# First attention stage: row-softmax results summed into the column-softmax bank by identity products, one copy and one output projection instead of two

## What is computed

```
w = (x @ W.T) split into heads; q, k, v = rms_norm(w) * g1, g2, g3
att   = q k^T / sqrt(d)
score = softmax(att, axis=-1) + softmax(att, axis=-2)
y     = score @ v, heads joined
x     = x + y @ W
```

## Time and profile before

| what | value |
|---|---|
| median of 3 runs | 331.37 us (329.57 to 331.48) |
| the profiled execution, its own time | 331.63 us |
| its span, first to last instruction | 329.6 us |
| around the span | 2.0 us |
| mean granted TensorE clock | 0.891 |
| block 1's loop in the span | about 46 to 145.4 us |

### The profile page before, as it was taken

How to read it: one execution, slowest core, us unless ns; L and a number is a source line. 1 busy time by engine, 2 the same in 40 slices (tenths; PEclk the granted TensorE clock), 3 DMA queues, 4 the chain that set the end, 5 groups by cost and what they waited for, 6 DMA issues and landing times.

```text
span 329.6 us, 6092 instructions
## 1 busy us (share of the span) xinstructions
PE 253.0 (77%) x2330; PEld 158.2 (48%) x2330; DVE 256.3 (78%) x495; ACT 205.1 (62%) x348; POOL 40.0 (12%) x65
## 2 busy tenths in 40 slices
PE   0045387697999979678779799879788987988755
PEld 0034163354655636354446556556445754565423
DVE  1989839667999998869968998995886577755771
ACT  3836648749989798844543864775308684574531
POOL 1201210111112112030100114511140000000000
PEclk9997555769999999997969859998969999999998
DMA  4933450543378564212030354363051000000000
GB/s 117 399 136 64 90 103 1 101 94 64 66 124 221 107 127 91 42 25 40 2 64 1 66 111 82 65 128 65 2 107 21 2 16 18 3 0 27 8 32 32
DMA packets 8524, 23.58 MB, mean 72 GB/s; under 512 B 1584, under 2 KB 2992, under 8 KB 8112
## 3 DMA queue, kind: packets, MB, share of 16 engines
q0 software_dynamic: 4320, 15.73, 25.5%
q1 hardware_dynamic: 4176, 7.48, 6.4%
HBM read 6.43 MB, written 1.05 MB: 23 GB/s over the span
## 4 chain that ended last, share of the span: by engine, by line
PE 48%; DVE 23%; issue 11%; ACT 10%; DMA 6%; POOL 1%; DVEq 0%; ACTq 0%; POOLq 0%
PE PS L1380 6%; PE PM L1225 4%; PE PO L1170 4%; PE PO L1185 3%; PE PS L1155 3%; DMA fwd<-bwd 3%; PE PM L1297 3%; DVE fwd L727 3%; PE PM L1115 3%; DMA fwd<-mid 3%; PE PO L1395 3%; DVE kp L972 3%; PE PO L1194 2%; PE PS L1473 2%; DVE bwd L735 2%
## 5 line engine op out<-in xcount | busy, mean ns | idle before, releaser
L530 ACT ACTIVATE E<-PS,negc,escale 128x1024 f32<-128x1024 f32 x32 | 38.1, 1198 | 9.8 <-PE PS L1155 9.7
L972 DVE TENSOR_REDUCE kp<-PS 128x2 f32<-128x256 f32 x64 | 32.3, 549 | 13.5 <-PE PS L1359 13.2
L653 ACT ACTIVATE E<-PS 128x384 f32<-128x384 f32 x64 | 27.8, 488 | 23.0 <-PE PS L1380 23.0
L1115 PE MATMUL PM<-w,sg 128*128 128x256 f32 x32 | 11.4, 517 | 24.8 <-DVE sg L750 24.8
L1155 PE MATMUL PS<-TP 32*128 32x256 f16 x256 | 21.4, 294 | 6.1 <-DVE TP L777 4.8
L330 POOL DMA_DIRECT2D fwd<-mid x15 | 13.0, 869 | 103.3 <-DVE fwd L727 103.3
L1170 PE MATMUL PO<-E,kp 128*32 128x256 f32 x256 | 20.6, 447 | 3.7 <-ACT E L530 1.8
L336 POOL DMA_DIRECT2D fwd<-bwd x15 | 12.9, 860 | 77.3 <-DMA fwd<-mid 47.8
L1115 PEld LDWEIGHTS PM<-w,sg 128*128 128x128 f32 x32 | 7.9, 261 | 27.1 <-DVE sg L750 25.7
L1185 PE MATMUL PO<-E,vr 128*32 128x256 f32 x256 | 19.5, 428 | 0.4 <-ACT yB L514 0.4
L735 DVE TENSOR_TENSOR_SCAN bwd<-ek,DT 128x511 f32<-128x511 f32 x16 | 19.8, 1234 | 0.0
(11 more groups left out here) (197 smaller groups left out, 583.9 us busy)
## 6 DMA issues: line engine op xcount, KB each, us to landing
fwd<-mid POOLq DMA_DIRECT2D x15, 512.0 KB, 4.6
fwd<-bwd POOLq DMA_DIRECT2D x15, 512.0 KB, 4.5
kT<-in_kT SPq DMA_DIRECT2D x4, 256.0 KB, 6.9
xT<-in_xT SPq DMA_DIRECT2D x4, 256.0 KB, 6.1
G<-in_w SPq DMA_DIRECT2D x1, 1024.0 KB, 9.1
vt<-in_w SPq DMA_DIRECT2D x1, 1024.0 KB, 10.9
G<-in_attn SPq DMA_DIRECT2D x1, 1024.0 KB, 6.9
out<-ek SPq DMA_DIRECT2D x8, 128.0 KB, 1.7
```

The costliest lines, as they stand in the source:

```text
L530: nc.scalar.activation(E[:, p % 6], PS[:, 2 * (p % 2):2 * (p % 2) + 2, :], ACT.Exp, bias=negc[:], scale=escale[:]).then_inc(S["e0_done"], 1)
L653: nc.scalar.activation(E[:, p % 4, i, 0:384], PS[:, i, 0:384], ACT.Exp, scale=QSCALE).then_inc(S["e1_done"], 1)
L972: nc.vector.tensor_reduce(kp[:, b % 2, u * H + 2 * j:u * H + 2 * j + 2, D], PS[:, at0:at0 + 2, lo:hi], AX, ALU.max, negate=True).then_inc( ...
L1115: ins = nc.tensor.matmul(PM[:, 0, u * C:(u + 1) * C], sg[:, seg(b, k * T + u * P, P)], w0[:, 0, k, :], start=(k == 0), stop=(k == HALF - 1))
```

## The change

The row part is no longer turned, copied and projected alone. ytok is laid out in the order of channels that the column part has in PO bank 1. After the second chunk of a region, `columns0` issues two identity products (ytok as the stationary operand, the identity as the moving one) that turn the row part and add it to that region. `turned_copy` then copies the sum, and one projection with the permuted W follows in slot 8b+5. Gone are `turn_y`, `yT_copy`, the first half of `project_both`, and the load of the half of w0 that it used. `links` now waits for the identity products that read its half of ytok one batch earlier (pv2_done) in place of the wait for turn_y.

```diff
-            sp.dma_start(w0[:], attn0_d).then_inc(S["ld_attn0"], 16)
+            sp.dma_start(w0[:, 0], attn0_d[:, 0]).then_inc(S["ld_attn0"], 16)
...
-                if j == 2 and 1 <= b <= B:
-                    yT_copy(b - 1, "ytr0_done", "out0_done", "yT0_done", gv[:])
...
-                if b >= 1 and c == 0:
-                    dve.wait_ge(S["ytr0_done"], b)
-                nc.vector.tensor_tensor(ytok[:, :, c * 64:(c + 1) * 64].rearrange("p u (g d) -> p u g d", g=4),
+                half = c // 2
+                if b >= 1:
+                    dve.wait_ge(S["pv2_done"], CH * (b - 1) + 2 * half + 2)
+                cols = ytok[:, :, half * P:(half + 1) * P].rearrange("p u (g e d) -> p u g e d", g=4, e=2)
+                nc.vector.tensor_tensor(cols[:, :, :, c % 2, :],
...
+                if q % 2 == 1:
+                    half = q // 2 % 2 * P
+                    pe.wait_ge(S["y0_done"], q + 1)
+                    for u in range(TT):
+                        ins = nc.tensor.matmul(PO[:, 1, at + u * P:at + (u + 1) * P], ytok[:, u, half:half + P], ident[:],
+                                               start=False, stop=(u == TT - 1), skip_group_check=True)
                 ins.then_inc(S["pv2_done"], 1)
...
-            def turn_y(b, done, wait):
...
-            def project_both(b, part):
...
+            def project_out(b):
+                pe.wait_ge(S["bc_done"], 2 * b + 2)
+                pe.wait_ge(S["qT0_done"], 4 * min(b + 2, B))
...
                 for o in range(HALF):
                     for k in range(HALF):
+                        ins = nc.tensor.matmul(PM[:, 1, o * T:(o + 1) * T], w0p[:, k, o * P:(o + 1) * P], yB[:, k, :],
                                                start=(k == 0), stop=(k == HALF - 1))
+                ins.then_inc(S["out0_done"], 1)
...
-                if j == 2 and 1 <= b <= B:
-                    turn_y(b - 1, "ytr0_done", [("y0_done", CH * b), ("qT0_done", 4 * min(b + 1, B))])
...
-                if j == 3 and 1 <= b <= B:
-                    project_both(b - 1, 0)
...
                 if j == 5 and 1 <= b <= B:
-                    project_both(b - 1, 1)
+                    project_out(b - 1)
```

More of the change, by code:

```diff
@@ L56 @@
     "proj0_done", "sq0_done", "ss0_done", "rs0_done", "k0_done", "ktr0_done", "kT0_done", "qT0_done",
-    "gains_done", "ln_bias", "qk0_done", "e0_done", "pv0_done", "y0_done", "ytr0_done", "yT0_done",
+    "gains_done", "ln_bias", "qk0_done", "e0_done", "pv0_done", "y0_done",
     "out0_done", "vcols_done", "rows0_done", "turned0_done", "pv2_done", "bc_done",
@@ L494, in kT_copy @@
                                      scale=gq[:]).then_inc(S["kT0_done"], 1)
[L496 to L501, removed]
             def rows_copy(q, bank, ready, used, done):
@@ L1186, in columns0 @@
                                                E[:, (2 * q + g // 2) % 6, g % 2, v * T:(v + 1) * T],
-                                               start=(q % 2 == 0 and v == 0), stop=(q % 2 == 1 and v == TT - 1),
-                                               skip_group_check=True)
+                                               start=(q % 2 == 0 and v == 0), stop=False, skip_group_check=True)
+                if q % 2 == 1:
[4 more added lines that the diff above has]
+                                               start=False, stop=(u == TT - 1), skip_group_check=True)
                 ins.then_inc(S["pv2_done"], 1)
@@ L1196, in turn_rows @@
                 ins.then_inc(S[done], 1)
-            def turn_y(b, done, wait):
[L1199 to L1208, removed]
+            def project_out(b):
+                pe.wait_ge(S["bc_done"], 2 * b + 2)
+                pe.wait_ge(S["qT0_done"], 4 * min(b + 2, B))
+                if b == 0:
+                    pe.wait_ge(S["ld_attn0p"], 16)
                 for o in range(HALF):
                     for k in range(HALF):
-                        ins = nc.tensor.matmul(PM[:, 1, o * T:(o + 1) * T], w[:, k, o * P:(o + 1) * P], yT[:, k, :],
+                        ins = nc.tensor.matmul(PM[:, 1, o * T:(o + 1) * T], w0p[:, k, o * P:(o + 1) * P], yB[:, k, :],
                                                start=(k == 0), stop=(k == HALF - 1))
-                ins.then_inc(S[done], 1)
-            def project_both(b, part):
[L1216 to L1229, removed]
+                ins.then_inc(S["out0_done"], 1)
             project0(0)
```

## The result

The changed kernel takes 332.59 us (median of 20 runs, 331.36 to 336.82) beside 331.04 for the kernel before; the ratio is 1.0059 (1.0034 to 1.0084). I had forecast 329.1. Measured once more, on another chip, it gave 331.48 and the ratio 1.0031 (0.9998 to 1.0064). The first measurement is clear of the noise, the second just not: the change is at best as fast as before and by the first measurement 0.6% slower, and it gives nothing of the forecast 0.7%. One slow run in each of the two measurements, of 336.82 and 457.58 us, is counted in the median and left out of the ratio.

A forecast was written before the change was run, and what follows sets the result against it. PE and DVE were both taken as nearly full, with DVE setting the pace; 0.14 + 0.1 + 0.5 + 0.45 + 1.06 = 2.25 us gained gave a median of 329.1 us. Forecast range 328 to 330; 8-in-10 range 326.7 to 331.9.

The forecast's parts named there:

- first copy: Start of the full run: with ACT's yT copy gone, the yc copy that DVE's wait hangs on comes 0.57 us earlier.
- identity products of slot 6: Slot 6, clock low: two identity products delay the whole chain by 0.43 us; bounds 0.22 and 0.6.
- full run: From 80.62 to 123.31 us: only DVE's gap of 0.11 can close, 0.1 us gained; removed projections there give nothing.
- links(11) to (12): DVE's wait of 1.06 us before 124.37 closes by 0.5; bounds 0 and 1.06.
- links(12) to (15): DVE's wait before 134.48 closes, 0.45 us, because the 1.83 us projection of batch 2 in slot 27 is gone.
- tail: After links(15): PE's side comes 1.46 us earlier, but only DVE's wait of 1.06 can close; the other 0.4 is given away.
- The spine: DVE's timeline taken as the spine of the sum: the block shortens by those DVE waits that the change closes.
- The rival in which PE is the bound: Each batch gives its 1.97 us of removed PE work, 7.9 in all, time 323.5; chance 0.07.
- slot-by-slot figure of 0.8: Following three engines from 80 us, turn_rows(12) comes about 0.8 us earlier while DVE is 0.24 earlier.
- two rivals: Clock falls in the tail, 330.6, chance 0.19; clock falls within the full run, 334.1, chance 0.07.
- the fourth rival: Slower: clock falls within the full run, a 10 us low stretch loses 5 us of PE work, 334.1; chance 0.07.

The follow-up runs named there:

- quiet profile of the changed kernel: Changed kernel measured again unaltered; its profile has no fall of the clock between links(4) and the last residual; 331.48 us, ratio 1.0031.
- late products: Changed kernel with the identity products moved one slot later, behind scores0 and turn_rows, with their own semaphore: 330.66 us, ratio 0.9980 to the kernel before.
- the best version: Changed kernel with identity products one slot later and unread f32 products in PE's gaps in slots 11, 25, 26, 33 and 36: 327.99 us, ratio 0.9916.
- changed kernel with all guards: Changed kernel, identity products in their place, plus unread f32 products in slots 11, 25, 26, 33 and 36: 331.59 us, ratio 1.0008.
- the other profile of the kernel before: Kernel before with unread f32 products added in slots 25 (two), 26 (one) and 33 (three): 332.50 us, ratio 1.0029.

## Why the prediction was wrong

Even without a fall of the clock the sum does not come out. The table sets its terms beside the quiet profile of the changed kernel, in us gained over the profile before:

| term | forecast | measured |
|---|---|---|
| first copy, links(3) to (4) | 0.57 | 0.58 |
| identity products of slot 6, links(1) to (2) | -0.43 | -0.79 |
| links(2) to (3) | none | 0.54 |
| full run, links(4) to (11) | 0.1 | 0.08 - 0.47 = -0.39 |
| links(11) to (12) | 0.5 | -0.64 |
| links(12) to (15) | 0.45 | 0.02 |
| tail, links(15) to residual | 1.06 | 0.84 |
| sum | 2.25 | 0.16 |

- **The spine.** That DVE, not PE, sets the pace from 80 to 120 us held. With late products links(4) to links(8) lasts 21.70 us beside 21.89, a gain of 0.19 where I had 0.1 for the whole run. PE is busy 20.80 us of it beside 21.58; in the kernel without identity products it is busy 19.95, and the stretch lasts 21.70 all the same. The rival in which PE is the bound is out.
- **The first copy.** links(3) to links(4) went from 7.38 us (73.24 to 80.62) to 6.80 in the changed profile (70.99 to 77.79): 0.58, with 0.57 forecast.
- **The identity products: this step failed.** I read the earlier trace rows as eight products and so took 0.22 us for two. They were four products of two instructions each, so a pair is 0.45, not 0.22; it measures 0.64 behind the narrow products and 0.54 behind turn_rows, so the switch, which I had in the upper bound of slot 6 alone, is taken to add the rest; that is an estimate from these three numbers. That makes 5.1 us in eight regions in place of 1.8. In slot 6 the price was not 0.43 but 0.79 (links(1) to links(2): 6.17 us before, 6.96 in the changed kernel's second profile). The low stretch from 65.00 that I named for it was the wrong one: columns0(1) had run from 59.21 to 60.92, in the low stretch before it, and in the second profile the pair takes 0.70 us (60.73 to 61.43) just as the clock comes back, at about 60.9. In the loop, products in place open 0.47 between links(8) and (11), where I had nothing. They keep the wait before links(14) at 0.42 to 0.43, where I had closed 0.45; with late products it does close (12 to 15 takes 13.68 us beside 14.36). The count of the removed projection was wrong in the same way (four products, not eight), but its time was taken from start to start, 1.83, and stood.
- **The wait before links(12): this step failed too.** I forecast that it closes by 0.5. Without a fall the stretch grew by 0.64 in the changed kernel and by 0.05 in the best version. It starts from ACT's exponential of slot 25, behind ACT's work for a gate layer, and ACT has no idle time before it from 113.92 us on in the changed profile, so work taken from PE can't bring it forward: the values of slot 26 start 1.88 us after links(11) before (119.60 to 121.48) and 1.89 in the quiet changed profile (119.28 to 121.17). From there PE has columns, pair, scores and turned rows in its queue, and links(12) comes 3.52 us later in place of 2.89: the difference is the pair, 0.65 (123.03 to 123.68). My slot-by-slot figure of 0.8 stood on no row that I showed.
- **The tail.** 15 to residual fell by 0.84, with 1.06 forecast. PE's side was to come 1.46 us earlier and so to have 0.4 to spare; it came 0.84 earlier. Of the missing 0.62, 0.53 are the pair, which takes 0.75 us up to the start of the copy (140.79 to 141.54 in the quiet profile) in place of 0.22.
- **The clock.** I made the sum without it and gave its falls 0.26 in two rivals. They came in most profiles of the unguarded changed versions. The changed kernel's own has two in the full run, as in the fourth rival, in stretches of about 4 us, not 10, and they cost 2.8 us together (67.04 - 64.26), not 5; other versions have stretches of 3 to 10 us. What the Trainium skill says in the place cited (TensorE: Matmul & The Clock Gate, What's actually happening), that the throttled state is the default and activity releases it, agrees with the fall at 119.8 us in a gap of PE and with the five profiles whose gaps were filled; it leaves open why the clock held in the same gaps in another execution. These falls come on top of a sum that was already used up.
- **Open.** The changed kernel with all guards is 3.0 to 3.6 us slower than the late version with the same guards. Their profiles account for 2.60 from links(1) on: 0.40 before links(4), 1.58 in the stretch, 0.62 after the residual. Only the 1.58 was taken apart; in the other two parts the clock differs from execution to execution. The 0.54 between links(2) and (3) in the table belongs there too: the other profile of the kernel before has 10.40 us there beside 10.19, and the changed one 9.59 and 9.65. What decides in which execution the clock falls in the same gaps was not found either.

## What to carry over

An f32 product was two instructions in these profiles: take its price from start to start of a whole group, and count products in the code, never by the x of a row. Where two engines are nearly full, ask of work removed from one what gaps it leaves, and whether its clock survives them; here the version that gained had its products one slot later and unread products put exactly into the gaps, eleven in all and some 5 us of PE time (an estimate, at 0.46 each by the four of 1.83 us). A product added in front of what another engine waits for costs what the slack there doesn't cover: the pair cost its whole 0.64 before links(12), about 0.1 in all from links(4) to links(8), and one slot later next to nothing in either place. Count the price of an added instruction against the slack of each place where it stands.

## What was not expected of the hardware

In one execution the clock fell some 0.6 us into the second of two gaps of 0.97 and 1.38 us, with about 1 us of work between them, and it stayed at 1.00 through the same gaps in another execution of the same kernel. With cheaper products (f16, 0.32 us a pair at the low clock, 123.38 to 123.70) the kernel was no faster than with f32 ones but slower (ratio 1.0105 beside 1.0059 and 1.0031), and its profile has a low stretch of some 10 us from the same gaps on.
